# First attention layer of a four-layer kernel: the masks of the natural scores move into DVE's maximum, and those of every second group of transposed scores into a DVE add in PSUM

## What is computed

```python
NUM_HEADS = 16; WINDOW = 128            # Dh = 16
q = apply_rope(proj(Wq, bq)) * Dh ** (-0.5)
k = apply_rope(proj(Wk, bk))
v = proj(Wv, bv)
scores = jnp.einsum('bhqd,bhkd->bhqk', q, k)
rel = idx[None, :] - idx[:, None]
blocked = (rel > 0) | (rel < -WINDOW)
scores = jnp.where(blocked[None, None], -jnp.inf, scores)
out = jnp.einsum('bhqk,bhkd->bhqd', jax.nn.softmax(scores, axis=-1), v)
```

## Time and profile before

| | |
|---|---|
| median of 3 runs | 2615.41 us (2611.98 to 2615.44) |
| profiled execution | 2620.68 us, span 2618.8 us |
| mean granted TensorE clock | 0.939 |
| busy share: PE, DVE, ACT, POOL | 84%, 55%, 38%, 34% |

### The profile page before, as it was taken

One profiled execution on the slowest core, in us unless ns is written; L12 is line 12 of the kernel. 1 busy time (PEld: TensorE's weight loads), 2 busy tenths in 40 slices (PEclk: granted clock), 3 DMA queues, 4 the chain that ended last, 5 costly groups with the idle time before them and its releaser, 6 DMA issues.

```text
span 2618.8 us, 42567 instructions
## 1 busy us (share of the span) xinstructions
PE 2206.4 (84%) x17140; PEld 1381.4 (53%) x17140; DVE 1430.5 (55%) x2527; ACT 994.5 (38%) x1449; POOL 899.5 (34%) x573
## 2 busy tenths in 40 slices
PE   2899999999999999588678689999378888888885
PEld 1444555555555555466556546776255555555553
DVE  2445554555555554446456445544566776677672
ACT  0133333333333333345334333334034554554443
POOL 4112222222222220103122122201338777877784
PEclk7799999999999999799989899999679999999997
DMA  6555555555556550456685841101454454446411
GB/s 132 101 113 115 106 122 106 106 116 113 114 111 118 111 108 26 147 193 246 227 287 190 285 137 65 49 19 55 138 140 109 125 156 128 128 105 165 120 44 49
DMA packets 226386, 328.86 MB, mean 126 GB/s; under 512 B 14368, under 2 KB 163984, under 8 KB 225936
## 3 DMA queue, kind: packets, MB, share of 16 engines
q1 hardware_dynamic: 219200, 321.56, 46.9%
q10 hardware_dynamic: 6992, 4.60, 0.6%
HBM read 197.53 MB, written 127.93 MB: 124 GB/s over the span
## 4 chain that ended last, share of the span: by engine, by line
PE 29%; DVE 12%; POOL 6%; DMA 5%; ACT 3%; issue 2%; SPq 1%; ACTq 0%; DVEq 0%; POOLq 0%
DVE l1f_rowmax L1785 4%; PE l1a_slot L1407 4%; POOL l1f_added L1665 4%; PE l1a_slot L1449 2%; PE l1a_slot L1398 2%; POOL l1f_added L1667 2%; PE l0f_slot L1108 2%; PE l1f_slot L1916 2%; DMA l0f_wide<-expert_outputs 2%; PE l0f_slot L1115 2%; PE l1f_os L1840 2%; PE l1f_slot L1907 2%; DMA l0f_x<-x 2%; DMA expert_outputs<-l0f_wide 1%; PE l0f_slot L1122 1%
## 5 line engine op out<-in xcount | busy, mean ns | idle before, releaser
L530 ACT ACTIVATE l0a_probs<-l0a_slot 128x1024 f32<-128x1024 f32 (+1 forms) x256 | 248.6, 972 | 335.9 <-PE l0a_slot L690 188.6
L587 DVE TENSOR_REDUCE l0a_rowmax<-l0a_slot 128x4 f32<-128x1024 f32 (+1 forms) x256 | 293.5, 1156 | 130.7 <-PE l0a_slot L700 127.8
L1735 ACT ACTIVATE l1f_probs<-l1f_slot 128x1024 f32<-128x1024 f32 x240 | 244.0, 1023 | 274.2 <-PE l1f_slot L1916 267.7
L1665 POOL TENSOR_TENSOR l1f_added<-l1f_probs 128x1024 f32<-128x1024 f32 x117 | 277.5, 2372 | 155.7 <-ACT l1f_probs L1735 155.7
L1785 DVE TENSOR_REDUCE l1f_rowmax<-l1f_slot 128x1 f32<-128x1024 f32 x240 | 287.3, 1217 | 66.8 <-PE l1f_slot L1907 66.3
L490 POOL TENSOR_TENSOR l0a_turned<-l0a_turned 128x512 f32<-128x512 f32 x32 | 40.8, 1274 | 557.9 <-DVE l0a_turned L573 557.9
L1916 PE MATMUL l1f_slot<-l1f_Qs,l1f_Ks 128*128 128x256 f32 x960 | 173.0, 304 | 37.9 <-DVE l1f_lo L1775 14.8
L1907 PE MATMUL l1f_slot<-l1f_Ks,l1f_Qs 96*128 96x512 f32 x480 | 177.9, 457 | 27.2 <-DVE l1f_rowmax L1785 18.1
L1916 PEld LDWEIGHTS l1f_slot<-l1f_Qs,l1f_Ks 128*128 128x128 f32 x960 | 145.3, 196 | 95.8 <-DVE l1f_rowmax L1785 32.7
L690 PE MATMUL l0a_slot<-l0a_mask,l0a_ident 128*128 128x512 bf16 (+1 forms) x512 | 150.3, 376 | 25.7 <-issue 23.3
L632 PE MATMUL l0a_O<-l0a_probs,l0a_V 128*32 128x128 f32 x3840 | 156.7, 279 | 11.2 <-issue 11.2
(11 more groups left out here) (193 smaller groups left out, 4015.0 us busy)
## 6 DMA issues: line engine op xcount, KB each, us to landing
expert_outputs<-l0f_wide SPq DMA_DIRECT2D x64, 512.0 KB, 3.3
l0f_wide<-expert_outputs SPq DMA_DIRECT2D x32, 1024.0 KB, 11.4
l0a_Qs<-qk_rows SPq DMA_DIRECT2D x96, 256.0 KB, 7.8
l0a_Ks<-qk_rows SPq DMA_DIRECT2D x96, 256.0 KB, 14.6
l1f_Ks<-kq_rows SPq DMA_DIRECT2D x48, 512.0 KB, 8.3
l0f_f<-in_dram SPq DMA_DIRECT2D x10, 2048.0 KB, 15.5
qk_rows<-l0a_hi SPq DMA_DIRECT2D x32, 512.0 KB, 2.8
qk_rows<-l0a_lo SPq DMA_DIRECT2D x32, 512.0 KB, 4.2
```

The source lines that it names most:

```text
L530: exp_ready.by(act.activation(probs[:, t % 2, HG * g:HG * g + HG, 0:reach, :], s[:, :, 0:reach, :], ACT.Exp, scale=SCALE))
L587: max_ready.by(dve.reduce_max(rowmax[:, t, :, 2 * g:2 * g + 2], s[:, :, :, first:2 * P], AX))
L1665: halved.by(pool.tensor_tensor(added[:, u, :], probs[:, 0, u, :], probs[:, 1, u, :], ALU.add))
L1735: exp_done.by(act.activation(probs[:, half, u - FIRST[b], :], s[:, :], ACT.Exp, scale=SCALE))
```

## The change

Every natural group loses its mask on PE. DVE reads the unmasked scores in four instructions of 256 elements (one for each head), each adding the mask, writing the sum back into PSUM and taking the maximum. Of the transposed groups, even ones keep the mask on PE; odd ones (every second) get it from a DVE add of 1024 elements in place in PSUM, and ACT waits for that add.

```diff
@@ scalar: tr
+                    if i % 2:
+                        masked.wait(act, X, i // 2 + 1)
@@ vector: nat, and new: tr
-                    max_ready.by(dve.reduce_max(rowmax[:, t, :, 2 * g:2 * g + 2], s[:, :, :, first:2 * P], AX))
+                    for half in range(2):
+                        for j in range(2):
+                            scores = s[:, half, j, first:2 * P]
+                            last = dve.tensor_tensor_reduce(scores, scores, visible[:, first:2 * P], 1.0, LOWEST, ALU.add, ALU.max,
+                                                            rowmax[:, t, half, 2 * g + j:2 * g + j + 1])
+                    max_ready.by(last)
+                if kind == "tr" and i % 2:
+                    s = by_pair(arrived(dve, X, step)).rearrange("p s j a q -> p (s j) a q")
+                    reach = 1 if n and i // NHG == BT - 1 else 2
+                    visible_from = maskT[:, 0:reach, :].unsqueeze(1).broadcast_to([P, HG, reach, P])
+                    masked.by(dve.tensor_tensor(s[:, :, 0:reach, :], s[:, :, 0:reach, :], visible_from, ALU.add))
@@ tensor: nat and tr
-                    mask_ends = bool(kind == "tr" and g % 2)
...
-                    if not mask_ends:
-                        add_mask()
+                    masked_here = kind == "tr" and g % 2 == 0
+                    if masked_here:
+                        for half in range(2):
+                            mm(o[:, half, :, reach, :], ident16[:, :], maskT[:, reach, :].unsqueeze(1).broadcast_to([P, 2, wide, P]),
+                               start=True, stop=False, skip_group_check=True)
...
-                    if mask_ends:
-                        last = add_mask()
```

More of the change, by code:

```diff
@@ L333, in window_attention_layer @@
     SCALE = float(DH) ** -0.5
+    LOWEST = -3e38
     CH = D // P
@@ L358, in window_attention_layer @@
         maskT = sb("maskT", [P, 2, P], bf16)
+        visible = mask[:, :, :].rearrange("p a n -> p (a n)")
         wq = sb("wq", [P, CH, D]); wk = sb("wk", [P, CH, D]); wv = sb("wv", [P, CH, D]); wo = sb("wo", [P, CH, D])
@@ L395, in window_attention_layer @@
         stacked = {w: signal(f"stacked_{w}", 6, 16) for w in "qk"}
-        max_ready = signal("max_ready", BT * NHG); maxT_ready = signal("maxT_ready", BT)
+        masked = signal("masked", BT * NHG // 2); max_ready = signal("max_ready", BT * NHG); maxT_ready = signal("maxT_ready", BT)
         placed = [signal(f"placed{t}", BT, 16) for t in range(2)]
@@ L551, in _ @@
             dve.memset(ln.half[:, :], -0.5).then_inc(setup, 1)
-            for s in (turned_ready, v_ready, max_ready, maxT_ready, recip_ready, ao_ready, summed):
+            for s in (turned_ready, v_ready, masked, max_ready, maxT_ready, recip_ready, ao_ready, summed):
                 s.start(dve)
@@ L678, in piece @@
                         reach = slice(0 if tile else 1, 2)
-                        rows, table, left, right = ROWS, mask, Qs, Ks
+                        rows, left, right = ROWS, Qs, Ks
                         moving = slice(P * (tile - 1 + reach.start), P * tile + P)
@@ L682, in piece @@
                         reach = slice(0, 2 if tile < NT - 1 else 1)
-                        rows, table, left, right = ROWS + 1, maskT, Ks, Qs
+                        rows, left, right = ROWS + 1, Ks, Qs
                         moving = slice(P * tile, P * (tile + reach.stop))
                     wide = reach.stop - reach.start
-                    mask_ends = bool(kind == "tr" and g % 2)
-                    def add_mask():
+                    masked_here = kind == "tr" and g % 2 == 0
+                    if masked_here:
                         for half in range(2):
[L690 to L693, removed]
-                    if not mask_ends:
-                        add_mask()
+                            mm(o[:, half, :, reach, :], ident16[:, :], maskT[:, reach, :].unsqueeze(1).broadcast_to([P, 2, wide, P]),
+                               start=True, stop=False, skip_group_check=True)
                     for j in range(2):
@@ L700, in piece @@
                             last = mm(o[:, half, j, reach, :].rearrange("p a q -> p (a q)"), left[r, 2 * g + j, here],
-                                      right[r, 2 * g + j, moving], start=mask_ends and not j, stop=not mask_ends,
+                                      right[r, 2 * g + j, moving], start=not masked_here, stop=True,
                                       skip_group_check=True, tile_position=(HALF * half, 0))
-                    if mask_ends:
-                        last = add_mask()
                 if kind == "maxT":
```

## The result

The changed kernel takes 2837.16 us (median of 4, 2812.37 to 2842.09) against 2615.43: ratio 1.083, 95% interval 1.077 to 1.090, 222 us more. I had forecast 2673, range 2612 to 2765: the direction was right, the time is outside.

What follows compares the result with a forecast made beforehand. PE bounds the first layer (busy 57.08 of 61.02 us a block). Rounds R0 to R3 sum to -0.5 + 1.5 - 1.0 + 3.2 = +3.2 us, +4.0 with full groups; mean 3.6 times 16 is 58, giving 2673 us, range 2612 to 2765.

Steps and rivals of the forecast that it cites:

- What one new instruction costs: DVE's fused add-and-maximum of 256 elements: spacing 0.365 us, short groups 0.232, ends 0.27 to 0.47.
- Phase A becomes DVE's: From a round's first pv to maxT (A), DVE needs 1.46 us a group, PE 1.00, so PE waits for DVE.
- s: Time after a round's first pv when DVE can begin the first natural group; 1.12 us at best.
- R3's A: Round R3, first pv to maxT: 8.92 us against 7.57, with R2's statistics and tr 3's add ahead on DVE.
- Phase B's chain: From maxT to the next round's first pv (B), tr 1's exponential waits for DVE's add; B 9.1, 9.15, 5.7, 10.4 us.
- R2's A: Round R2, first pv to maxT: 7.27 us, with DVE starting at 1.3 after tr 3's add.
- Rival 3: PE's clock falls in its new idle time: at 0.88 some 4 us more a block, 2737 us; chance 0.05.
- Rival 4: Delays on DVE are absorbed and rounds keep PE's saving: 2567 to 2590 us; chance 0.14 together with rival 5.
- Rival 5: The new DVE instruction costs under 0.308 us, near streaming: 2576 to 2612 us; chance 0.14 together with rival 4.
- Rival 1: A cheap new DVE instruction, spacing about 0.34 us: 2641 to 2650 us; chance 0.14.
- Rival 2: A dear new DVE instruction, spacing 0.42 to 0.47 us: 2726 to 2780 us; chance 0.12.
- rival 6: No change in the kernel's time, loss and gain cancel: 2610 to 2621 us; chance 0.05.

Runs made afterwards that it cites:

- e11: Changed kernel plus throwaway PE matmuls: two before each natural group, two before tr 0, six before tr 2, six in R1's back step; 2739 us, ratio 1.047.
- e6: Kernel before, with only natural group 0 of R0, R2 and R3 masked by DVE's fused maximum; 2596 us, ratio 0.991.
- e7: Kernel before, with natural groups 0 and 1 of R0, R2 and R3 masked by DVE's fused maximum; 2581 us, ratio 0.986.
- e4: PE as in the changed kernel, DVE and ACT as in the kernel before, so no masking at all; 2579 us, ratio 0.985.
- e2: Changed kernel with only its natural half: DVE's fused maxima, all transposed masks on PE, no DVE add; 2750 us, ratio 1.050.

## Why the prediction was wrong, by its own steps

- **What one new instruction costs: right, within its range.** I took a spacing of 0.365 (short 0.232); measured 0.382 and 0.249. By the prediction's own 10 us for each 10 ns that adds 17 us: 2690.
- **Phase A becomes DVE's: right.** In the R3 shown, the fused maximum of nat 0 starts at s = 2.54 (546.09 after a first pv at 543.55); 2.54 + 16 x 0.382 + 0.13 = 8.8, measured 8.81. The mean of R3's A is 9.15, forecast 8.92, or 9.19 with the measured spacing.
- **Phase B's chain: right at full clock.** e11 has B of 9.04, 9.21 and 10.42 in R0, R1, R3, where I wrote 9.1, 9.15 and 10.4, and R2's 7.19 less six throwaway matmuls (1.3) is 5.9 for 5.7. R2's A is mis-sized: 8.4 for 7.3 (7.5 with the measured spacing). In e11 two throwaway matmuls ahead of nat 0 are 0.5 of that, and before them PE waits 0.34 us for an exponential that holds the slot. So some 0.4 a block, 6 us, is the prediction's, by this estimate.
- **The clock: the step that failed.** The sum has no term for the clock: it takes every piece of PE's work at 1.00. Rival 3 had the mechanism and I gave it 0.05, with "The idle stretches stay short, so I give it little", and sized it at a clock of 0.88 and 64 us. The clock fell to 0.74, in the R3 shown with no wait over 2 us before the fall, and it cost some 140 us (next item). I reasoned from single gaps and from a stretch of the second layer with 1.00 at 72% busy; but that stretch has another pattern of work. In the changed layer PE's work in phase A lies in pieces of 0.4 to 1 us between waits. The row with 0.88 stood beside the other and was the better guide.
- **The sizes.** Of the 222 us, the clock's share is at least some 95 to 98: the changed kernel less e11, which has more PE work (98 by the medians, 95 by the ratios). By phase B, the changed kernel less e11 is 2.5, 2.0, 2.3 (filler taken off) and 1.9: 8.7 a block, 139 us. The rest, 83 to 124 us, is what DVE's and ACT's chains cost, forecast at 58, or 75 with the measured spacing. The lower end is the likelier: e11's block of 69.4 less the filler on its path (0.5 in R0's A, 0.5 in R2's A, 1.3 in R2's B) is 67.1, which is 5.2 over the kernel before, or 83 us, an estimate.
- **The other rivals.** Rivals 4 and 5 (faster): the delays were not absorbed (R3's A is 9.2, where rival 4 needed under 7.6), and the spacing is above 0.308. Rivals 1 (0.34) and 2 (0.42 and more) are out by the spacing too, and rival 6 by the time.

## What to carry to other kernels

Here, work taken off TensorE gave its time where the granted clock held (e6 and e7), and less than half of it or nothing where the clock fell (e4, e2). So price what runs next at the lower clock as well, as a rival with a real chance, even where each new wait is short. Hand an engine work where it idles anyway and stop before it becomes the phase's bound: the same fused maximum for two groups of four gave 1.4%, for all four in every round it cost 5% (e2), and with half the transposed masks besides 8%. Where an engine's average share shows room, look phase by phase, and at what stands before the new instruction in its queue.

## What the runs showed of the hardware

The granted clock fell from 1.00 to 0.50 at 554 us, after 8 us in which PE was busy 4.38 us in pieces, with waits of 0.97 and 1.94 us, none long. Throwaway matmuls brought the layer from 0.74 to 0.99 and the time down by 98 us. In e2 the same phase B of R0 took 8.83 us at 1.00 and 11.71 at 0.65.

The fused add-and-maximum shows as two rows, the operation and a read of the accumulator (an internal sum or maximum) of 0.14 us that starts with the next operation. The spacing is 0.382 us for 256 elements and 0.249 for 128: 1.04 ns an element and 0.116 an instruction, where a plain add has 0.334 at 256. The write back into PSUM is within that; for the plain add of 1024 elements it shows no cost (1.226 in place in PSUM, 1.225 with its output in SBUF). The section of the Trainium skill that the prediction drew on ("Vector Engine (DVE) Microarchitecture Reference", 5.2) has some 75 ns an instruction, and the plain add's rows lie near it with 67; the fused one pays some 40 ns more than the section's figure here. Which of its parts costs that, the accumulator's read or another, is not shown.
